# Issuing the spread of a block's reciprocals as four DMAs, one for each head

## What is computed

```
scores = einsum('bhqd,bhkd->bhqk', q * scale, k)
attn   = softmax(scores, axis=-1)
o      = einsum('bhqk,bhkd->bhqd', attn, v)
```

## Time and profile before

| | us |
|---|---|
| median of 3 runs | 491.04 (490.61 to 492.54) |
| profiled execution, its own time | 494.82 |
| profiled execution, span of the trace | 493.1 |
| busy: TensorE, VectorE, ScalarE, GpSimd | 466.7, 361.7, 270.3, 209.7 |
| mean granted clock of TensorE | 0.975 |

### The profile page before, as it was taken

The page is one execution under the profiler, slowest core; times in us unless marked ns, Lnnn a source line. Parts: engine busy times, 40 slices in busy tenths (PEclk is TensorE's granted clock), DMA queues, the critical chain, the costliest instruction groups (busy, mean ns, idle before and its releaser), DMA issues.

```text
span 493.1 us, 7075 instructions
## 1 busy us (share of the span) xinstructions
PE 466.7 (95%) x2252; PEld 239.9 (49%) x2252; DVE 361.7 (73%) x684; ACT 270.3 (55%) x518; POOL 209.7 (43%) x195
## 2 busy tenths in 40 slices
PE   8899999999899889999999979989999999999996
PEld 6554444443337656544444423547544444433463
DVE  7799888885653679987777717659998677848673
ACT  3228777776602425876766646033777676866032
POOL 8200031108110003899788950000788788990100
PEclk9959999999897999999999989999999999999999
DMA  5231432103200054587963551015547875353002
GB/s 151 55 60 23 142 57 47 23 5 64 56 10 1 0 122 110 102 193 160 183 155 72 94 93 23 1 48 137 116 104 155 175 148 104 61 101 60 2 2 85
DMA packets 20369, 40.70 MB, mean 83 GB/s; under 512 B 7426, under 2 KB 8586, under 8 KB 20204
## 3 DMA queue, kind: packets, MB, share of 16 engines
q1 hardware_dynamic: 15036, 24.23, 21.0%
q0 software_dynamic: 5152, 16.00, 17.5%
q10 hardware_dynamic: 144, 0.02, 0.0%
HBM read 4.76 MB, written 1.05 MB: 12 GB/s over the span
## 4 chain that ended last, share of the span: by engine, by line
PE 68%; DVE 8%; SPq 8%; DMA 5%; ACT 4%; POOL 4%; issue 3%; ACTq 0%; DVEq 0%; POOLq 0%
PE S L955 16%; PE PV L993 14%; PE S L982 14%; PE S L1107 4%; SPq L326 4%; SPq L319 4%; DVE max L716 3%; POOL SUMS L505 3%; DMA SUMS<-SUMS 3%; PE M L1006 3%; PE PV L907 2%; DMA k_stack<-kL 2%; ACT E L569 2%; PE PV L933 2%; DVE SUMS L747 2%
## 5 line engine op out<-in xcount | busy, mean ns | idle before, releaser
L716 DVE TENSOR_REDUCE max<-S 128x1 f32<-128x512 f32 x384 | 238.9, 674 | 10.9 <-PE S L955 10.2
L569 ACT ACTIVATE E<-S 128x512 f32<-128x512 f32 x384 | 211.0, 605 | 57.0 <-PE S L982 49.6
L505 POOL TENSOR_TENSOR SUMS<-E 128x512 f32<-128x512 f32 x120 | 159.0, 1441 | 121.1 <-ACT E L569 117.6
L955 PE MATMUL S<-k_stack,q_stack 126*128 126x512 f32 x384 | 177.5, 478 | 6.9 <-DMA k_stack<-kL 4.5
L982 PE MATMUL S<-q_stack,k_stack 128*128 128x512 f32 x384 | 155.8, 418 | 5.4 <-ACT E L569 4.6
L955 PEld LDWEIGHTS S<-k_stack,q_stack 126*128 126x128 f32 x384 | 73.3, 193 | 77.5 <-DVE max L716 47.8
L993 PE MATMUL PV<-E,V 128*32 128x512 f32 x768 | 91.6, 598 | 0.0
L982 PEld LDWEIGHTS S<-q_stack,k_stack 128*128 128x128 f32 x384 | 73.2, 193 | 34.8 <-ACT E L569 19.6
L729 DVE TENSOR_TENSOR mHL<-S,mHL 4x128 fp32r<-4x128 f32 x48 | 13.3, 278 | 48.2 <-ACT mHL L558 48.2
L993 PEld LDWEIGHTS PV<-E,V 128*32 128x32 f32 x768 | 20.6, 109 | 46.6 <-issue 26.5
L558 ACT ACTIVATE mHL<-S 4x128 fp32r<-4x128 f32 x48 | 12.7, 264 | 50.2 <-PE S L973 50.2
(11 more groups left out here) (176 smaller groups left out, 339.5 us busy)
## 6 DMA issues: line engine op xcount, KB each, us to landing
SUMS<-SUMS POOLq DMA_DIRECT2D x30, 512.0 KB, 6.1
k_stack<-kH SPq DMA_DIRECT2D x28, 128.0 KB, 3.4
q_stack<-qH SPq DMA_DIRECT2D x40, 64.0 KB, 2.0
rec_sb<-den_sb SPq DMA_DIRECT2D x9, 256.0 KB
q_stack<-qH SPq DMA_DIRECT2D x16, 128.0 KB, 2.4
k_stack<-kL SPq DMA_DIRECT2D x14, 128.0 KB, 4.2
q_stack<-mHL SPq DMA_DIRECT2D x96, 2.0 KB
k_stack<-kH SPq DMA_DIRECT2D x22, 64.0 KB, 2.3
```

The lines of the kernel that those rows point to most:

```text
L505: pool.tensor_tensor(SUMS[:, slot, :], E[:, E_PLAN[s][0], :], E[:, E_PLAN[s + 1][0], :], ALU.add).then_inc(sum_ready, 1)
L569: act.activation(E[:, slot, :], B[:, ring_of_scores(s) % B_RING, :], ACT.Exp, scale=1.0 if l == 0 else float(HEAD_DIM[l]) ** -0.5).then_in ...
L716: dve.tensor_reduce(max8[:, m % 2, 2 * t + half:2 * t + half + 1], A[:, n % A_RING, :], AX.X, ALU.max, negate=True).then_inc(a_used, 1)
L955: pe.matmul(A[:, n % A_RING, :], q_stack[0:SHIFT_ROW, slot, q0:q0 + P], k_stack[0:SHIFT_ROW, slot, k0:k0 + HALF], start=True, stop=True).t ...
```

## The change

The one DMA of `spread_reciprocals`, whose source is four rows each repeated 32 times and whose destination is all 128 partitions of rec_sb, becomes four DMAs. Each has one row of den_sb as its source, repeated 32 times, and 32 partitions of rec_sb as its destination. All four increment the same semaphore, so the two waits on it count four times as much. The bytes copied are the same.

```diff
                 sp.wait_ge(recs_rows, 16 * (FOLDED * l + b + 1))
                 sp.wait_ge(att_ready, FOLDED * l + b)
                 sp.wait_ge(att_tail, 2 * l)
-                sp.dma_start(rec_sb[:, :],
-                             den_sb[0:P:DP, :].rearrange("u (o n) -> u o n", o=1)
-                             .to_broadcast([HEADS_B, DP, HALF])).then_inc(recs_spread, 16)
+                for u in range(HEADS_B):
+                    sp.dma_start(rec_sb[DP * u:DP * (u + 1), :],
+                                 den_sb[DP * u:DP * u + 1, :].rearrange("u (o n) -> u o n", o=1)
+                                 .to_broadcast([1, DP, HALF])).then_inc(recs_spread, 16)
...
             def normalise(l, b):
...
-                pool.wait_ge(recs_spread, 16 * (FOLDED * l + b + 1))
+                pool.wait_ge(recs_spread, 16 * HEADS_B * (FOLDED * l + b + 1))
...
             def denominators_out(l, b):
...
-                act.wait_ge(recs_spread, 16 * (FOLDED * l + b))
+                act.wait_ge(recs_spread, 16 * HEADS_B * (FOLDED * l + b))
```

## The result

The changed kernel takes 499.46 us in the median of four runs (495.51 to 501.89), the kernel before 491.79 beside it: a ratio of 1.014, interval 1.009 to 1.019. The forecast was 487.2, faster. The sign is wrong. The time lies within the range, but only in the part that was drawn for the second rival (494 to 504), so the range was met by another mechanism than the forecast's. The profiled execution of after took 499.53 us, with a span of 497.8.

A forecast was written before the change was run, and what follows sets the result against it. TensorE, busy 95% of the span, was taken as the bound, with one late sums' transfer stalling layer 1: 2.56 + 1.30 = 3.86 us. All else 0, so 491.04 - 3.86 = 487.2 us; 8-in-10 range 486.0 to 501.5.

The forecast's parts named there:

- the second rival: Spread: one row feeds 16 engines no faster than one; late multiplications and sums, together 13 us, 504 us; chance 0.25.
- the spread's bounds: Last block's spread, first issue to use: 3.7 us from below, 12.3 from above; about 4 taken, against 7.0 before.
- three rows at 438.2: Spread in the old trace: three rows at once took 0.083 us each, 25 GB/s, read as sources not limiting.
- steady 49 GB/s: Old spread running alone: share 0.24, 3.8 engines, 0.16 us a row, 5.3 us for 256 KB.
- Sync's three more issues, taken as 0: Sync's queue: 3 x 0.56 = 1.7 us more per spread, nine times, taken as hidden; up to 1.7 us if not.
- cover of 2.9: Sync's queue, layer 1: gap between the spread's issue ending at 275.99 and the next instruction at 278.89, covering 1.7 us.
- The stall of layer 1: Denominators wait 2.56 us for the sums' transfer, then lose 1.30 at low clock; removing it was to gain 3.86 us.
- The first rival: No change: the profiled execution is 3.78 us above the runs' median, almost exactly the stall; 491 us, chance 0.28.
- GpSimd's wait for block 0's spread: GpSimd, layer 1: a 1.25 us wait expected to go, so additions come earlier and the sums' transfer gains margin.
- deciding point: Last multiplication against output projection: costs begin when the spread is used 3.2 us later; just past it, 494 us.
- The third rival: The four do not spread: a one-row transfer stays on one engine, 10.6 us of data, about 500 us; chance 0.07.

The follow-up runs named there:

- second profile of before: The kernel before, unchanged, profiled once more: 491.94 us, with no wait at the denominators of layer 1.
- third profile of before: The kernel before, unchanged, profiled yet again after one earlier repeat: 489.81 us, with no wait at the denominators of layer 1.
- four for block 1: Two kernels against before: the spread issued as four transfers for block 1 only (493.93 us, ratio 1.006), or for blocks 1 and 2 (495.76 us, 1.010).
- other source rows: Kernel before, still one transfer, but reciprocal rows on partitions 0, 36, 72, 108 instead of 0, 32, 64, 96: 491.75 us, ratio 0.9996.
- four transfers by columns: Against before, four transfers, each a quarter of the columns of all four rows, so each stays on four engines: 494.71 us, ratio 1.006.
- block 2 alone: Against before, four transfers for the spread of block 2 only, the last of each layer: 491.63 us, ratio 1.000.
- block 1 alone: Against before, four transfers for the spread of block 1 only, one for blocks 0 and 2: 493.93 us, ratio 1.006.

## Why the prediction was wrong

**Where the time went.** From the two scores ahead of the denominators to the output projection, an undisturbed layer takes 20.8 us: 438.81 to 459.65 in layer 2 of before, 285.24 to 306.08 and 435.99 to 456.81 in the second profile of before. After takes 309.95 - 283.34 = 26.6 in layer 1 and 464.36 - 439.50 = 24.9 in layer 2, 5.8 and 4.0 more. Together 9.8; after reached layer 1's scores 1.9 us earlier than that profile did, which leaves 7.9, against 7.6 us between the spans (497.8 and 490.2). A third profile of before reached them at 283.6, so the 1.9 is no gain of the change.

**The step that failed** is the choice between the spread's bounds, 3.7 and 12.3 us. The prediction took about 4, because three rows at 438.2 took 0.083 us at once, "so the sources were not what held them to half the rate". They were: with the rows in other places the same four engines move 99 GB/s. Stretches of after with one spread alone:

```profile
91.00:93.00 2.00, 2.00 (x19) 0.71 (x18) 1.91 (x4) 1.37 (x3) 0.00 (x0) 1.00 0.88 27
...
94.00:95.00 1.00, 1.00 (x6) 0.63 (x4) 0.87 (x3) 0.75 (x3) 0.00 (x0) 1.00 0.63 64
```

Sixteen engines are at work (share 0.88) and move 27 GB/s: 27 / (0.88 x 16) = 1.9 GB/s each, over 1 us for a row of 2 KB. All of them read one source row or, where the first two transfers overlap, rows 0 and 32. Where it comes to 64 the second and third transfer overlap, rows 32 and 64. So the spread is used 9.4 us after its first issue, between the bounds and nearer to the upper one. A rate read off a few hundredths of a microsecond in a busy stretch was set against the steady 49 GB/s of four whole microseconds, and the steady row had it right. The Trainium skill ("SBUF — State Buffer", Door 1: The DMA port swizzle) puts partitions 0 and 32 on one port and 64 and 96 on another, with 36, 72 and 108 on three more; the prediction cited it and let the rows at 438.2 overrule it. The runs agree with it for reads, all but the rows at 438.2: 49 GB/s from two such pairs, 99 from four rows on four ports, 27 from one row.

**Sync's three more issues, taken as 0,** are the second failed term. The prediction gave each its old 0.56 us and hid 1.7 us under a cover of 2.9. Four issues take 3.17 us where no sums' transfer is under way. Beside one they took 7.56 us in layer 1 of after and 3.68 in layer 2, and 7.68 to 9.01 in the kernels with four for block 1; the cover is then gone. This was bounded at "up to 1.7 us a spread, on shift rows for which TensorE does not wait there"; TensorE did wait, 3.21 us, and the clock behind that made it 5.8.

That the late issue made the shift rows late is argued, not shown. There is a rival: their data may have stood behind the spread's. By the packets in after's trace the first data of these shift rows moves at 286.2, 4.1 us after their issue at 282.09, as the spread ends (its fourth transfer, issued at 280.90, lands after 6.0 us, at 286.9). By those in the second profile of before it moves at 283.8, 4.5 us after the issue at 279.31, and the spread ends at 286.1. An earlier issue would then have helped little: at 27 GB/s the four rows take 256 KB / 27 = 9.7 us (an estimate), whenever they are issued, and the failed term would be the first one again. No run tells the two apart.

**The stall of layer 1.** The forecast that the sums' transfer would come in time was right: issued at 275.35, it landed after 8.1 us, at 283.4, ahead of the denominators at 284.26. But the kernel as it usually runs has no stall there, so the gain was only for the profiled execution. The first rival said so; the other profiles of before, and the kernel with other source rows (no stall, same time), bear it out. The prediction's objection, that the order of the two issues is the same in every execution, was wrong: Sync came first by 0.07 us in the execution with the stall (12.7 us to landing), GpSimd in the one without (8.7). In layers 1 and 2 of all traces with one transfer for block 1 and the old rows it goes that way: Sync first in three cases, 11.1 to 12.7 us; GpSimd first in seven, 8.7 to 9.3. No version forced the order, so that it is the cause is likely, not shown.

**The second rival** had most of the mechanism of layer 2: block 0's multiplication holds GpSimd's queue, the sums' transfer goes out late, the denominators stall with a low clock behind. It gave 434.6 for the issue and 4.0 + 1.3 us of stall; it was 432.21 and 2.58 + 1.37 (3.29 - 1.92), since the spread is 2.4 us later and not 5.3. Lateness is only a part of it. Without the stall the denominators would start 8.3 us after the issue (443.08 - 2.58 = 440.50, against 432.21; in before it was 10.4, 429.33 to 439.72), and the transfer also takes longer, 10.7 us beside the four instead of the 9.1 that the rival kept. The four transfers by columns show that it needs both: there the issue is as late (428.50, with the denominators at 436.67), the transfer lands after 7.2 us, and nothing stalls. In layer 1 the rival had the landing at 289.9, where it was 283.4; but GpSimd's wait for block 0's spread there, which the prediction's sum let vanish, grew from 1.25 us to 2.57. The last multiplication, 2.4 us later, stays inside the rival's deciding point of 3.2, and no projection waits: right, and shown by the kernel with block 2 alone. Its time for "just past the deciding point" was 494; what it lacked was Sync.

**The third rival** (four that do not spread) is out: shares near 1 show all sixteen engines at work.

**What stays open.** Why the issues of Sync get so long beside the sums' transfer was only seen, not tried apart. Open too is why the scores wait 0.81 to 0.89 us for a shift row in three cases and over 3 us in two. The time of its issue does not decide it: the second shift row is issued about 8.5 us after the spread's first issue both in layer 1 with block 1 alone (284.69 - 276.14, wait 0.85) and in layer 1 of after (282.93 - 274.48, wait 3.21). How three rows could take 0.083 us at 438.2 is open as well. That a pair's other engine was busy with the sums' packets explains it for one pair at most, since three of four engines were at it. No version tried beats the kernel before.

## What to carry to other kernels

Count the source rows of a broadcast before counting the engines: here sixteen engines on one row moved 27 GB/s and four engines on four well-placed rows 99. Before pricing a stall that stands in one profile, hold the profiled time against the median: if the difference is the size of the stall, the stall is probably not in the median. And price one more issue on a queue by its time in the busiest stretch where it will stand, and follow what is queued behind it, its data too; nothing waited at once for the multiplication or for the shift rows, but the sums behind the one and the scores behind the other were wanted a few microseconds later.

## What the runs showed of the hardware

A single row of 2 KB feeds 27 GB/s to sixteen engines; sixteen rows eight partitions apart, 167 GB/s. A DMA issue on Sync that takes 0.56 us alone took up to 4.3 us as one of four while a transfer of 512 KB was on its way (one of after's):

```profile
L371 SPq DMA_DIRECT2D rec_sb<-den_sb x36: 568/592/4315, 89.0 to 457.1; - x36
```

(The columns are the shortest, median and longest issue in ns.) And one transfer of 512 KB beside the same spread, in the same place of the same kernel, landed after 8.7 us in one execution, where it was issued 0.07 us ahead of the spread, and after 12.7 in another, where it was issued 0.07 us behind.
